# A selective-scan kernel with a routed gate: three chunk ends reordered, one gather table for both batches, one scratch row moved

## The reference, cut to what matters

```python
xn = layernorm(x)                                   # x: 2 x 1024 tokens of 512
proj = xn @ W_in.T; x_, gate = split(proj, 1024)
x_ = silu(conv_b + sum_j conv_w[:, j] * shifted(x_, j))
ts, Bm, Cm = rms(each of split(x_ @ W_x.T, [32, 16, 16]))
dt = softplus(ts @ W_dt.T + b_dt);  A = -exp(A_log)
state = state * exp(dt * A) + (dt * x_) * Bm        # over 1024 steps, 1024 channels x 16 states
y = (sum_n state * Cm + x_ * D) * silu(gate);  s = y @ W_out.T
g = silu(two of 8 experts per token, weighted by a softmax over the two)
out = x + s * g
```

## Time and profile before

| | us |
|---|---|
| median of 3 runs | 1105.64 (1104.69 to 1107.46) |
| the profiled execution | 1104.69 |
| its span, first to last instruction | 1102.9 |
| busy: DVE | 1025.4 (93%) |
| busy: POOL | 903.4 (82%) |
| busy: PE | 874.1 (79%) |
| busy: ACT | 730.4 (66%) |
| DMA, mean over the span | 199 GB/s |

### The profile page before, as it was taken

The page is one execution under the profiler, slowest core; times in us unless marked ns, Lnnn a source line. Parts: engine busy times, 40 slices in busy tenths (PEclk is TensorE's granted clock), DMA queues, the critical chain, the costliest instruction groups (busy, mean ns, idle before and its releaser), DMA issues.

```text
span 1102.9 us, 10140 instructions
## 1 busy us (share of the span) xinstructions
PE 874.1 (79%) x2722; PEld 318.7 (29%) x2722; DVE 1025.4 (93%) x1052; ACT 730.4 (66%) x1284; POOL 903.4 (82%) x353
## 2 busy tenths in 40 slices
PE   5954377898879998888855868889897999778577
PEld 3331022333323332333211323333322333223122
DVE  6759999999999989999999989899999989999997
ACT  2664666777766666777665767678777666576565
POOL 0019998988969898989999968798797988998895
PEclk9986678999989999999966879999899999799789
DMA  9345377656577566566743363865457656665714
GB/s 328 117 154 201 106 221 232 216 201 227 181 258 250 184 230 219 177 201 178 241 155 128 140 200 115 313 223 189 158 205 271 228 198 228 220 220 181 268 38 152
DMA packets 78089, 219.26 MB, mean 199 GB/s; under 512 B 15824, under 2 KB 17232, under 8 KB 71376
## 3 DMA queue, kind: packets, MB, share of 16 engines
q1 hardware_dynamic: 58096, 166.67, 43.7%
q10 hardware_dynamic: 12672, 31.46, 7.4%
q0 software_dynamic: 7264, 20.47, 6.7%
HBM read 176.85 MB, written 41.72 MB: 198 GB/s over the span
## 4 chain that ended last, share of the span: by engine, by line
DVE 36%; PE 22%; POOL 14%; issue 12%; DMA 8%; ACT 6%; SPq 1%; DVEq 0%; ACTq 0%; POOLq 0%
DVE sc_ps L1131 18%; POOL drive L541 8%; DVE drive L1131 6%; PE x_ps L1421 5%; DVE drive L1141 3%; DMA rep<-rep_rows 3%; PE x_ps L1284 3%; PE f_ps L1374 3%; POOL drive L554 3%; PE y_ps L1389 3%; DMA x_slot<-xn_rows,slot_tok 2%; PE dt_ps L1349 2%; DVE x_ps L1072 2%; PE sc_ps L1284 2%; ACT sc_ps L760 1%
## 5 line engine op out<-in xcount | busy, mean ns | idle before, releaser
L541 POOL TENSOR_TENSOR drive<-rep,b_all 128x2048 f32<-128x2048 f32 x128 | 580.5, 4539 | 119.4 <-DVEq L1015 77.5
L760 ACT ACTIVATE sc_ps<-rep,a_neg 128x512 f32<-128x512 f32 x512 | 331.8, 681 | 87.5 <-DVE drive L1141 58.9
L1131 DVE TENSOR_TENSOR_SCAN sc_ps<-sc_ps,state,drive 128x512 f32<-128x512 f32 x180 | 220.8, 1273 | 5.9 <-ACT sc_ps L760 5.9
L1141 DVE TENSOR_TENSOR drive<-sc_ps,c_all 128x1024 f32<-128x1024 f32 x180 | 220.4, 1224 | 6.2
L1389 PE MATMUL y_ps<-drive,stack 128*32 128x512 f32 x1024 | 157.0, 691 | 85.3 <-DVE drive L1141 60.3
L1131 DVE TENSOR_TENSOR_SCAN sc_ps<-sc_ps,drive 128x512 f32<-128x512 f32 x180 | 210.0, 1212 | 2.2 <-ACT sc_ps L760 1.2
L554 POOL TENSOR_TENSOR drive<-drive,c_all 128x1024 f32<-128x1024 f32 x76 | 179.5, 2362 | 20.5 <-ACT state L739 14.9
L1374 PE MATMUL f_ps<-w_ring,xT_slot 128*128 128x512 f32 x368 | 173.2, 614 | 14.4 <-ACT xT_slot L772 14.4
L1349 PE MATMUL dt_ps<-xnT,w_g 128*128 128x512 f32 x232 | 122.6, 677 | 22.1 <-ACT dtu L727 22.1
L1374 PEld LDWEIGHTS f_ps<-w_ring,xT_slot 128*128 128x128 f32 x368 | 70.1, 198 | 118.4 <-issue 118.3
L1131 DVE TENSOR_TENSOR_SCAN drive<-sc_ps,state,drive 128x512 f32<-128x512 f32 x76 | 93.1, 1266 | 2.8 <-ACT sc_ps L760 2.8
(11 more groups left out here) (184 smaller groups left out, 1058.6 us busy)
## 6 DMA issues: line engine op xcount, KB each, us to landing
rep<-rep_rows SPq DMA_DIRECT2D x128, 512.0 KB
w_ring<-wring SPq DMA_DIRECT2D x46, 1024.0 KB
rep_rows<-dtu ACTq DMA_DIRECT2D x32, 512.0 KB, 3.2
slot_rows<-y_slot ACTq DMA_DIRECT2D x46, 256.0 KB, 4.4
w_g<-wg_in SPq DMA_DIRECT2D x32, 256.0 KB
w_x<-wx_in SPq DMA_DIRECT2D x24, 256.0 KB
xn_rows<-rep SPq DMA_DIRECT2D x16, 256.0 KB, 2.7
b_all<-bc_rows SPq DMA_DIRECT2D x16, 256.0 KB, 4.6
```

The lines of the kernel that those rows point to most:

```text
L541: pool.tensor_tensor(drive[:, m % RING, :, :], rep[:, n % 2, :, 1, :], b_all[:, q:q + 1, :].broadcast_to([P, NR, TC]), ALU.mult).then_inc( ...
L760: act.activation(sc[:, r, :], rep[:, n % 2, r, 0, :], ACT.Exp, scale=a_neg[:, lo:lo + 1]).then_inc(decay_ok, 1)
L1131: dve.tensor_tensor_scan(to, sc[:, r, :], drive[:, m % RING, r, :], state[:, lo:lo + 1] if follows else 0.0, ALU.mult, ALU.add).then_inc(s ...
L1141: dve.tensor_tensor(drive[:, m % RING, 2 * h:2 * h + 2, :], sc[:, 2 * h:2 * h + 2, :], c_all[:, q:q + 1, :].broadcast_to([P, 2, TC]), ALU. ...
```

## The change: what it does

Three edits.

1. The two tables of `SLOT_STEPS` become one, that of batch 1, used for both batches. In batch 0, tile 2 loses its first slot, slots 0 to 12 each come half a tile later, and tile 8 gains a second slot.
2. At the three chunk ends, DVE takes the step sizes of the next tile after `high(m)` and `gate_tile(n - 1)`; ACT takes `keep_dt` behind `decays(m + 1, 1)` and `keep_rows` behind `copy_slot_T`; SP issues B row 3 right behind B rows 0 to 2, ahead of C row 0.
3. `r1` moves from `x_ps` to SBUF (16 free columns of `moe`), and its reduction over two values becomes an addition (`tensor_tensor`).

```diff
-SLOT_STEPS = ({2: (0, 1), 3: (2, 3), ..., 7: (10, 11), 8: (12, None), 9: (13, 14), ...},
-              {2: (None, 0), 3: (1, 2), ...})
+SLOT_STEPS = {2: (None, 0), 3: (1, 2), ..., 7: (9, 10), 8: (11, 12), 9: (13, 14), ...}
@@ scan_moe
+        r1 = spare[1][:, 448:464]
-        m1, r1 = x_ps[:, 3 * P:3 * P + 16], x_ps[:, 3 * P + 16:3 * P + 32]
+        m1 = x_ps[:, 3 * P:3 * P + 16]
@@ SP
                 if chunk_end:
                     store_rows(c + 1)
-                    for q in range(NQ - 1):
+                    for q in range(NQ):
                         spread_b(c + 1, q)
                     spread_c(c + 1, 0)
...
                 if chunk_end:
-                    spread_b(c + 1, NQ - 1)
                     spread_c(c + 1, 1)
@@ ACT
                 decays(m + 1, 0)
-                if chunk_end:
-                    keep_dt(n + 1)
-                    keep_rows(n + 1)
                 if early is not None:
                     copy_x(NT * (c + 1) + early)
                 decays(m + 1, 1)
+                if chunk_end:
+                    keep_dt(n + 1)
                 copy_slot_T(b, first_slot)
+                if chunk_end:
+                    keep_rows(n + 1)
@@ DVE
-                link(dve.tensor_reduce(r1, e_both.rearrange("p k t -> p t k"), AX_X, ALU.add))
+                link(dve.tensor_tensor(r1, e1, e2, ALU.add))
...
+                rms_behind = t == NT - 1 and c < NCH - 1
                 if n:
                     low(m)
-                    if pe_log(n + 1):
+                    if not rms_behind and pe_log(n + 1):
                         times_x(n + 1)
-                    elif chunk_end:
-                        step_sizes(n + 1)
                     high(m)
                 if n:
                     gate_tile(n - 1)
+                if chunk_end and pe_log(n + 1):
+                    times_x(n + 1)
+                elif chunk_end:
+                    step_sizes(n + 1)
```

More of the change, by code:

```diff
@@ L40 @@
 POOL_QUADS = {n: (0, 1) if n in (1, 15) else (0, 1, 2) for n in range(TILES) if 2 <= n % (PER_ROW * NT) < 14 or n in (1, 15)}
-SLOT_STEPS = ({2: (0, 1), 3: (2, 3), 4: (4, 5), 5: (6, 7), 6: (8, 9), 7: (10, 11), 8: (12, None), 9: (13, 14), 10: (15, 16), 11: (17, 18), 12: (19, 20), 13: (21, 22)},
-              {2: (None, 0), 3: (1, 2), 4: (3, 4), 5: (5, 6), 6: (7, 8), 7: (9, 10), 8: (11, 12), 9: (13, 14), 10: (15, 16), 11: (17, 18), 12: (19, 20), 13: (21, 22)})
+SLOT_STEPS = {2: (None, 0), 3: (1, 2), 4: (3, 4), 5: (5, 6), 6: (7, 8), 7: (9, 10),
+              8: (11, 12), 9: (13, 14), 10: (15, 16), 11: (17, 18), 12: (19, 20), 13: (21, 22)}
 LATE_PUTS = [(2, 0), (2, 2), (11, 2), (12, 0), (12, 2), (13, 0), (13, 2), (13, 3)]
@@ L57, in slots_at @@
 def slots_at(c, t):
-    return SLOT_STEPS[c // PER_ROW].get(NT * (c % PER_ROW) + t, (None, None))
+    return SLOT_STEPS.get(NT * (c % PER_ROW) + t, (None, None))
 def early_x(c, t):
```

## The result

The changed kernel takes 1118.5 us, median of four timed runs (1115.9 to 1121.1), against 1105.4 us for the kernel before on the same chip; the ratio is 1.0115 with a 95% interval of 1.0085 to 1.0147. In us of before that is +12.7 (+9.4 to +16.2), where I had forecast +1.0. The profiled execution took 1122.5 us, its span 1120.6, 17.7 us above the span of before's.

The account below looks back on a forecast made before the run. DVE, busy 93% of the span, was taken as the bound. Terms +1.0 + 0 - 0.9 + 2.9 - 2.0 = +1.0 us gave 1105.7 on the profiled execution, 1106.6 against the median; 8-in-10 range 1100.2 to 1111.4.

Parts of the forecast that it names:

- r1: Four instructions on 16 columns, once in the program: 0 us, ends -0.7 and +0.3.
- Tile 7: Chunk end: 0.9 us of DVE's bracket lie ahead of PE's and POOL's limits, so -0.9 us, ends -2.4 and +2.3.
- the same pattern: Tile 7 was taken to behave as tile 23, now with the same slots, its bracket 0.9 us longer.
- Tile 15: Chunk end: late `rep` passes through POOL to DVE in tile 17, d - 0.9: +1.0 us, ends -2.3 and +1.7.
- d: How much later `rep` is in tile 15: between 1.3 (half the issue shift) and 2.6 us, taken as 1.9.
- Tiles 23 to 25: POOL 0.7 us late, transfers round the gather 0.7 us early, nothing gained or lost: 0, ends -1.5 and +3.2.
- The slot in tile 8: Four more transposes and products on PE, as tile 24 has: +2.9 us, ends 0 and +4.3.
- second rival: `rep` behind B row 3 on SP's blocked queue delays POOL, then DVE: +5.7 us, 1111.3, chance 0.22.
- Tile 2: First slot goes, fewer transfers bring the second slot's rows earlier, DVE's two brackets shrink: -2.0 us, ends -2.3 and 0.
- third rival: Tile 2 gains nothing, its rows landing at 171.6 whatever stands in the queue: +3.0 us, 1108.6, chance 0.08.
- rival one: DVE's brackets at the chunk ends and in tile 2 go, nothing replaces them: -5.2 us, 1100.4, chance 0.27.
- its sign: Sign of the blocked queue: new DVE brackets before the first low scans of tiles 8, 16 or 24, released by POOL's drives.

Follow-up runs that it names:

- ends: All three chunk-end edits of the change (issue of B row 3, order on ACT and DVE) alone, on the kernel before: 1.0082 of before (1.0055 to 1.0110).
- order: Only the chunk-end order on ACT and DVE, on the kernel before, SP issuing as before: 1.0023 of before (1.0000 to 1.0045).
- nosp: The changed kernel with one thing undone, B row 3 issued behind `rep` again: 1.0059 of before (1.0036 to 1.0081).
- v_ring: The kernel before with the 1 MB of weights of batch 0's slot 1 issued near 143 instead of at 160: 1.0014 of before (0.9989 to 1.0039).
- r1: Only the r1 edit (r1 in SBUF, its sum a tensor_tensor), on the kernel before: 1.0015 of before (0.9992 to 1.0037).
- slots: Only the slot table edit, on the kernel before: 1.0044 of before (1.0019 to 1.0069).
- after: The changed kernel with all three edits, against the kernel before: 1118.5 us, 1.0115 of before (1.0085 to 1.0147).
- p_op: The kernel before with r1 left in PSUM and its sum made a tensor_tensor of two SBUF operands: 1107.5 us in one run.
- p_place: The kernel before with r1 moved to SBUF and its sum left a reduction with one SBUF operand: 1110.0 us in one run.
- sp: Only SP's issue order at the chunk ends, B row 3 ahead of C row 0 and `rep`, on the kernel before: 1.0045 (1.0022 to 1.0068).

## Why the prediction was wrong

The measured time, 1118.5, lies above the whole range of the prediction (1111.4 at most). Point by point, with the terms of the prediction:

- **r1, forecast 0 (-0.7 to +0.3): wrong, and outside its ends.** The step that failed is "none can take longer than the gate's 0.68 us on 512 columns". It bounded the instruction by its size and did not ask what its operands share with another engine. It stands 4.15 us, 3.9 more than the reduction took; tile 1 hides 2.6 of them; 1.3 us are left.
- **Tile 7, forecast -0.9: wrong in sign.** `rep` was issued 3.2 us later after the rms, as forecast, but the step that failed is that, in "the same pattern" as tile 23, nothing of it would reach DVE: POOL was 1.9 us late. The gate of tile 7 is 0.1 to 0.2 us later, and tiles 8 and 9 take 4.5 us instead of the slot's 2.9. +1.7 in all. In ends, without the slot, the same stretch from 5 to 9 is +1.8.
- **Tile 15, forecast +1.0: the mechanism right, d mis-sized.** I took d as 1.9, "nearer to none of the two" ends 1.3 and 2.6. POOL's first drives are 3.7 us later in both traces (22.1 to 25.8). Put into the prediction's own d - 0.9 this is +2.8, and the gates from 13 to 17 step by 3.0 and 2.2. The cap of 2.6 was wrong: the issue itself moved by 3.0, and `rep` then took longer still, 9.3 to 9.7 us from its issue to POOL's drives in the five traces with B row 3 in front, against 8.9 in before and 8.7 in order. By the rule cited in the prediction, that descriptors of one queue start in the order of issue (the Trainium skill, "DMA: Bandwidth & Descriptors", section "Two DMAs through the same engine are not ordered"), d would have been 3.2, and 3.7 with the issue shift as it was measured, which is what the traces show. But nosp, without the row in front, also takes 9.4 us, so no run isolates the row's bytes as the cause.
- **Tiles 23 to 25, forecast 0 (-1.5 to +3.2): wrong.** Failed step: "with the 8.9 us of tile 15, `rep` had landed by 840.5". In the kernels in which POOL waits for `rep` there, its drives start 10.0 to 10.8 us after the issue in tile 23 (10.8 and 10.7 in the changed kernel), against 9.6 in tile 15: the interval of one stage was carried to another. By these intervals before had about 1 us of slack, not 2.5. The shift, "3.2 us later, as in tile 7", was carried over too. In tile 23 of before POOL's last drives of the chunk end at 833.73:

```profile
829.21 4.52 POOL L541 TENSOR_TENSOR drive<-rep,b_all 128x2048 f32<-128x2048 f32 x1
```

With three issues behind that, the first `rep` issue would have been near 835.5, 4.0 us later and not 3.2; it was 4.1 and 3.4 us later. POOL's lateness was 3.5 and 2.7 us, not 0.7, and the stage cost +5.8 and +2.5 us. The second rival priced this at +2.0.

- **The slot in tile 8, forecast +2.9: right** (2.9 and 2.8).
- **Tile 2, forecast -2.0: not there, as far as the traces can tell.** The step that failed is that a MB less in the queue brings the rows in earlier. They land at 172.2 (171.6 and 173.7 in the two traces of before), as the third rival had it; the forecast was read from one trace at a place that moves by 2 us from one execution to the next. v_ring says the same with another MB. Tile 3 is where a later landing comes out, up to 5.9 us; it does so in the kernel before too.
- **The brackets, rival one: they do go**, all three; but VectorE's 93% was no promise of gain. Rival two, the blocked queue, is what happened: its place and path are right, and its sign came, DVE brackets of 2.51 and 3.21 us before the first low scans of tiles 8 and 24, released by POOL's drives. Its price of 1111.3 was too low: it too had tile 2 at -2.0 and r1 at 0, and less than was measured for tiles 15 and 23 to 25.

Put together, 1.3 for r1, 1.7 for tile 7, 3.0 or 2.2 for tiles 15 to 17, 5.8 or 2.5 for tiles 23 to 25, 2.9 for the slot and nothing for tile 2 give 14.7 us by the first trace of the changed kernel and 10.6 by the second, round the measured 12.7. The parts measured alone, r1 +1.7, slots +4.9 and chunk ends +9.1, sum to 15.7, each with 2.5 to 3 us on either side. The median of all runs and one pair of traces differ too: the first trace of before is near the fastest of its runs, and of the 17.7 us between the two spans about 5 are such differences.

## What to carry to other kernels

A bracket on the busiest engine is worth closing only with work that was ready, and without sending later what the engine produces next: the high scans alone, put into the gap, and the small loads put behind `rep` gave -5 us (the scans alone 1.8, not clear of 0), where gate and product in front of the step sizes gave +2.5. On an issue queue that runs in order, do not put a transfer whose buffer comes free late in front of one that an engine waits for; one such row at three places cost 5 to 6 us here. And look for every added instruction at where both of its operands lie and what GpSimd is doing at that time, before calling it free.

## What the hardware showed that I had not expected

- A VectorE tensor_tensor of 128x16 with both operands in SBUF stood 3.7 to 4.15 us, until GpSimd's running tensor_tensor ended (after, r1, p_op, p_place); with one operand in PSUM it took 0.17 us beside the same GpSimd work (before), and with both in SBUF behind it 0.17 us (r1). It came in the last of GpSimd's four multiplications each time (4.5 us each).
- In tile 15 a 2 MB load with 256 KB issued in front of it on the same queue took 0.4 to 0.8 us longer from issue to first use than the 8.9 us of before; one kernel without the 256 KB in front (nosp) took 0.5 us longer as well, so the bytes are not shown to be the cause. A megabyte taken from right behind such a load in tile 2 gained nothing (1.0014, 0.9989 to 1.0039).
- In tile 2 GpSimd's drives, which wait for `rep`, started at 170.14 and 172.44 in the two traces of before and at 174.19 in sp, whose program is the same up to there; `rep` was issued at 156.89, 157.44 and 157.89. So 1 of the 4 us was there at the issue, and 3 are the transfer's. One tile later up to 4 us of difference between such traces shows in DVE.
